# Attention head outputs turned on VectorE instead of TensorE, with part of the normalisation on GpSimd

## The reference, cut to what matters

```python
scores = jnp.einsum('bhqd,bhkd->bhqk', q, k) * SCALE      # 512 x 512 for each head
attn = jax.nn.softmax(scores, axis=-1)
out = jnp.einsum('bhqk,bhkd->bhqd', attn, v)
out = out.transpose(0, 2, 1, 3).reshape(B, Tq, C)
return out @ Wo.T + bo                                    # added to x
```

## Time and profile before

| | |
|---|---|
| median of 3 runs | 4522.98 us |
| the runs | 4522.26, 4527.35, 4522.98 us |
| span of the profiled execution | 4527.3 us |
| PE / DVE / ACT / POOL busy | 3886.3 / 3074.1 / 2057.9 / 795.1 us |
| steps of a0 (first to last exponential) | from 163.8 us to about 760 us |
| steps of a2 | from 2977 to 3393 us |
| steps of a3 | from 3836 to 4250 us |

### The profile page before, as it was taken

One profiled execution on the slowest core, in us unless ns is written; L12 is line 12 of the kernel. 1 busy time (PEld: TensorE's weight loads), 2 busy tenths in 40 slices (PEclk: granted clock), 3 DMA queues, 4 the chain that ended last, 5 costly groups with the idle time before them and its releaser, 6 DMA issues. The chain is left out here.

```text
span 4527.3 us, 83053 instructions
## 1 busy us (share of the span) xinstructions
PE 3886.3 (86%) x30431; PEld 2824.0 (62%) x30525; DVE 3074.1 (68%) x7110; ACT 2057.9 (45%) x3636; POOL 795.1 (18%) x510
## 2 busy tenths in 40 slices
PE   6799997799377999796399999779997987999899
PEld 5344443798365777575378888635555665555577
DVE  7666664456746666544566666678867887888587
ACT  3355554233103333342044444347775762777510
POOL 6433321401431000000023322410000013000000
PEclk9799999599668999897599999879998998999999
DMA  8233331201311000011054544722210015222000
GB/s 266 86 100 101 101 91 54 68 26 42 125 62 33 19 19 19 28 40 37 13 158 124 132 125 125 230 80 66 66 38 19 1 35 199 60 67 67 28 19 19
DMA packets 234478, 338.02 MB, mean 75 GB/s; under 512 B 39204, under 2 KB 132950, under 8 KB 234167
## 3 DMA queue, kind: packets, MB, share of 16 engines
q1 hardware_dynamic: 218280, 306.66, 21.4%
q0 software_dynamic: 15888, 27.23, 2.8%
HBM read 242.42 MB, written 107.01 MB: 77 GB/s over the span
## 5 line engine op out<-in xcount | busy, mean ns | idle before, releaser
L1918 ACT ACTIVATE a_pT<-a_psS 128x512 f32<-128x512 f32 x1536 | 836.0, 597 | 387.7 <-PE a_psS L1804 382.4
L1990 DVE TENSOR_REDUCE a_mx<-a_psA 128x1 f32<-128x512 f32 x1024 | 656.4, 685 | 82.9 <-PE a_psA L1782 82.8
L1819 PE MATMUL a_psZ<-a_pT,a_V 128*17 128x128 f32 x12288 | 488.8, 278 | 0.0
L1782 PE MATMUL a_psA<-a_ks,a_qs 48*128 48x512 f32 (+1 forms) x1536 | 405.5, 523 | 83.8 <-DVE a_mx L1990 36.9
L1986 DVE CUSTOM_DVE_ANT_0 a_scored<-a_psA,a_hide_q 128x512 bf16<-128x512 f32 x512 | 332.7, 688 | 184.4 <-PE a_psA L1782 183.3
L1819 PEld LDWEIGHTS a_psZ<-a_pT,a_V 128*17 128x17 f32 x12288 | 272.8, 97 | 272.7 <-issue 163.3
L1782 PEld LDWEIGHTS a_psA<-a_ks,a_qs 48*128 48x128 f32 (+1 forms) x1536 | 151.6, 192 | 330.2 <-DVE a_mx L1990 127.7
L1804 PE MATMUL a_psS<-a_qs,a_ks 50*128 50x512 f32 (+1 forms) x1536 | 318.3, 408 | 2.7 <-ACT a_pT L1918 0.8
L3262 DVE SCALAR_TENSOR_TENSOR ex_h<-ex_psU,ex_ub,ex_sg 128x512 f32<-128x512 f32 x129 | 96.9, 751 | 189.3 <-PE ex_psU L159 182.3
L2002 POOL TENSOR_TENSOR X<-X,a_osb 128x512 f32<-128x512 f32 x48 | 61.1, 1278 | 935.3 <-ACT a_osb L1905 917.3
L3208 ACT CAST ex_w_h<-X 128x1024 fp32r<-128x1024 f32 x102 | 106.0, 1040 | 149.5 <-DMA X<-in_L_ffn_gw 145.7
(11 more groups left out here) (606 smaller groups left out, 10227.2 us busy)
## 6 DMA issues: line engine op xcount, KB each, us to landing
a_qs<-a_q_parts SPq DMA_DIRECT2D x576, 64.0 KB, 2.3
a_ks<-a_k_parts SPq DMA_DIRECT2D x576, 64.0 KB, 2.3
a_k_parts<-a_p_kp SPq DMA_DIRECT2D x96, 256.0 KB, 2.6
a_q_parts<-a_p_qp SPq DMA_DIRECT2D x96, 256.0 KB, 3.2
X<-in_L_ffn_gw SPq DMA_DIRECT2D x36, 512.0 KB, 4.4
X<-in_L_ffn_up_w SPq DMA_DIRECT2D x36, 512.0 KB, 3.3
X<-in_L_ffn_down_w SPq DMA_DIRECT2D x36, 512.0 KB, 3.8
top_rows<-blank_rows SPq DMA_DIRECT2D x32, 514.0 KB, 4.8
```

What stands on the lines that cost most here:

```text
L1782: nc.tensor.matmul(psA[:, unit(a, par) % 3], qs[r, g % ring, p % 2, q * P:(q + 1) * P], ks[r, g % ring, p % 2], start=True, stop=True).the ...
L1819: last = nc.tensor.matmul(psZ[q * VP:q * VP + VW, g % 2, j * P:(j + 1) * P], V[:, b, kt, g % NG * GH + j, :], pT[:, p % 2, par, kt, q * P: ...
L1918: nc.scalar.activation(pT[:, p % 2, par, kt, :], psS[:, unit(t, par) % 3], ACT.Exp).then_inc(exp_done, 1)
L1990: nc.vector.tensor_reduce(mx[:, p // 2 % 2, par, p % 2, q:q + 1], psA[:, unit(a, par) % 3], AX_X, ALU.max).then_inc(a_used, 1)
```

## The change

The output of a group is turned by one VectorE transpose of 32x32 blocks, straight out of the `psZ` bank into SBUF (`ohT`). ACT's copy and PE's four transposes go, and with them the entry "heads" in `found`. So that a block transpose leaves each query on a partition of its own, the four column groups of `values` no longer take four runs of 128 queries: group q takes the queries i * 128 + q * 32 + c (i from 0 to 3, c from 0 to 31), four runs of 32 queries, through `tokens_of`. `take_output` runs at the same place as before (`TAKEN` = 5, ahead of the maxima of step 8g + 13). It has the transpose first; in a2 and a3 it keeps the reciprocal, and the product goes to POOL (`normalise`). In a0 the four operations stay on DVE and read SBUF instead of PSUM. New semaphores: `o_turned` (the bank is read; PE waits for it before it reuses the bank) and `on_ready` (the product is done; the "turn" waits for it, and DVE before the next transpose).

```diff
+TAKEN = TB + 1
-        oh = sb("oh", [P, GH, P])
+        ohT = sb("ohT", [P, GH, TB, VP])
-            found.append((STEPS * g + 12, STEPS * g + 12, "heads", g))
+        def tokens_of(x, q):
+            return x.rearrange("p (i q c) -> p q i c", i=TB, q=TB)[:, q]
+        def turned_before(t):
+            return max(0, min(GROUPS, (t - STEPS - TB) // STEPS + 1))
 # PE, values(t)
+                        if g >= 2:
+                            pe.wait_ge(o_turned, g - 1)
...
-                                                    pT[:, p % 2, par, kt, q * P:(q + 1) * P], start=(kt == 0), stop=(kt == TB - 1),
+                                                    tokens_of(pT[:, p % 2, par, kt], q), start=(kt == 0), stop=(kt == TB - 1),
 # PE, use(...)
+                    if t == first and turned_before(t) > 0:
+                        pe.wait_ge(o_turned, turned_before(t))
-                    elif what == "heads":
-                        pe.wait_ge(oh_ready, n + 1)
-                        for j in range(GH):
-                            last = nc.tensor.transpose(ps[:, j * P:(j + 1) * P], oh[:, j, :], G.ident[:])
                     elif what == "turn":
...
+                        pe.wait_ge(on_ready, NG * (u + 1))
 # ACT
-                        nc.scalar.copy(oh[:].rearrange("p j c -> p (j c)"), psZ[:, g % 2]).then_inc(oh_ready, 1)
 # DVE
+                def take_output(g):
+                    dve.wait_ge(o_done, GH * (g + 1))
+                    if g > 0:
+                        dve.wait_ge(on_ready, g)
+                    nc.vector.transpose(ohT[:].rearrange("p j i v -> p (j i v)"), psZ[:, g % 2]).then_inc(o_turned, 1)
+                    got = ohT[:, :, :, 0:VW]
                     if hidden is not None:
...
                         link(nc.vector.tensor_tensor(oraw[:], usum[:, u % 2, :, heads, :].rearrange("p q j v -> p j q v"), weight, ALU.mult))
+                        dve.wait_ge(o_turned, g + 1)
+                        link(nc.vector.tensor_tensor(oraw[:], oraw[:], got, ALU.add))
+                        got = oraw[:]
+                    else:
+                        dve.wait_ge(o_turned, g + 1)
+                    nc.vector.reciprocal(rden[:], got[:, :, :, DH]).then_inc(rden_ready, 1)
+                    if hidden is None:
                         return
                     dve.wait_ge(rden_ready, g + 1)
+                    nc.vector.tensor_tensor(of_heads, got[:, :, :, 0:DH], rden[:].unsqueeze(3).to_broadcast([P, GH, TB, DH]), ALU.mult
+                                            ).then_inc(on_ready, 1)
 # POOL
+                def normalise(g):
+                    pool.wait_ge(rden_ready, g + 1)
+                    nc.gpsimd.tensor_tensor(of_heads, ohT[:, :, :, 0:DH], rden[:].unsqueeze(3).to_broadcast([P, GH, TB, DH]), ALU.mult
+                                            ).then_inc(on_ready, 1)
+                if hidden is None:
+                    for g in range(GROUPS):
+                        normalise(g)
+                        if g >= NG and g % NG == 0:
+                            add_output(2 * (g // NG) - 2)
+                            add_output(2 * (g // NG) - 1)
```

More of the change, by code:

```diff
@@ L1707, in attention_by_pairs @@
         a_ready, s_ready = [sem("a_ready0"), sem("a_ready1")], [sem("s_ready0"), sem("s_ready1")]
-        a_used, max_ready, exp_done, o_done, oh_ready, rden_ready, x_full, x_free = (
-            sem(n) for n in ("a_used", "max_ready", "exp_done", "o_done", "oh_ready", "rden_ready", "x_full", "x_free"))
+        a_used, max_ready, exp_done, o_done, o_turned, rden_ready, on_ready, x_full, x_free = (
+            sem(n) for n in ("a_used", "max_ready", "exp_done", "o_done", "o_turned", "rden_ready", "on_ready", "x_full", "x_free"))
         if hidden is not None:
@@ L1891, in _ @@
                                 if n >= 4:
-                                    act.wait_ge(x_free, number["heads", n - 4] + 1)
+                                    act.wait_ge(on_ready, n - 3)
                                 nc.scalar.activation(e0[:, n % 4], mx[:, n % 2].rearrange("p r j q -> p (r j) q"), ACT.Exp,
@@ L1896, in _ @@
                             if n >= 2 * TB:
-                                act.wait_ge(x_free, number["heads", NG * (n // TB - 2) + NG - 1] + 1)
+                                act.wait_ge(on_ready, NG * (n // TB - 1))
                             nc.scalar.copy(usum[:, n // TB % 2, n % TB], bank_of(k)[:, 0:H * VW].rearrange("p (h v) -> p h v", h=H)
@@ L1943, in split_maxima @@
                                                    ALU.subtract).then_inc(max_ready, 1)
-                def take_output(g, k):
+                def take_output(g):
                     u, heads = g // NG, slice(g % NG * GH, (g % NG + 1) * GH)
-                    dve.wait_ge(x_full, k + 1)
-                    got = bank_of(k).rearrange("p (j q v) -> p j q v", j=GH, v=VP)
+                    of_heads = on[:, u % 2].rearrange("p i (h d) -> p h i d", h=H)[:, heads]
+                    dve.wait_ge(o_done, GH * (g + 1))
[3 more added lines that the diff above has]
+                    got = ohT[:, :, :, 0:VW]
                     if hidden is not None:
@@ L1970, in _ @@
                         split_maxima(t // STEPS + 1)
-                    for what, n, k in ending(t - 1, "heads"):
-                        take_output(n, k)
+                    g = t // STEPS - 1
+                    if t % STEPS == TAKEN and 0 <= g < GROUPS:
+                        take_output(g)
                     a = t + LEAD
@@ L2002, in add_output @@
                     nc.gpsimd.tensor_tensor(tiles, tiles, osb[:, n % 2].rearrange("p (q d) -> p q d", q=2), ALU.add).then_inc(out_added, 1)
-                for u in range(B):
-                    if hidden is not None and u + 1 < B:
+                def normalise(g):
+                    u, heads = g // NG, slice(g % NG * GH, (g % NG + 1) * GH)
+                    of_heads = on[:, u % 2].rearrange("p i (h d) -> p h i d", h=H)[:, heads]
+                    pool.wait_ge(rden_ready, g + 1)
[7 more added lines that the diff above has]
+                            add_output(2 * (g // NG) - 1)
+                for u in range(B if hidden is not None else 0):
+                    if u + 1 < B:
                         pool.wait_ge(x_free, number["sums", TB * u + TB - 1] + 1)
```

10 lines of the change are left out of this document (removed).

## The result

Six runs of each kernel, side by side: 4547.15 us median for the changed kernel (4541.17 to 4550.63), 4527.71 us for the kernel before (4522.26 to 4536.67). The ratio is 1.0041, 95% interval 1.0029 to 1.0053, so 13 to 24 us slower. The profiled execution spans 4541.3 us, 14.0 us more than that of before. (The median of before over six runs is 4.7 us above that of the three shown ahead of the prediction. The difference measured beside it is 19.4 us; the prediction had 29.)

The account below looks back on a forecast made before the run. DVE's stay at each group's output was taken as the bound; 12.8 us in a2 and a3 plus 17.6 in a0 minus 1 at the ends gave +29 us on 4522.98, so 4552 us, range 4520 to 4585.

Parts of the forecast that it names:

- What bounds: At each group's output in all three attentions, DVE ends PE's wait; removing PE's transposes and ACT's copy counts nothing.
- The transpose: On DVE, the added block transpose of 128x512 out of PSUM takes 0.69 us, bounded by 0.42 and 1.22 us.
- a2 and a3: the term: DVE's time for a group's output in a2 and a3 rises from 0.73 to 0.93 us: 12.8 us over 64 groups.
- a0: 0.55 us forecast: In a0 the transpose comes in front of DVE's four operations, each group 0.55 us later: 17.6 us over 32 groups.
- POOL's product: In a2 and a3 the product moved to POOL takes 0.74 us and no turn waits for it.
- The ends: At the three attention ends, the path from last values to turn shortens by 0.3, 0.3 and 0.7 us: about -1 us.
- The sum: Whole kernel: 12.8 + 17.6 - 1 = +29 us, 4552 us predicted.
- (a): Faster: PE is the bound in a0, saving 0.30 us a group there, 9.6 us: 4513 us; chance 0.12.
- (b): No change: DVE's transpose runs at twice the rate, 0.42 us: 4526 us; chance 0.10.
- (c): Slower than forecast: DVE's transpose runs at half the rate, 1.22 us; 80 us more, 4603 us; chance 0.08.
- (d): PE's values matmuls pay 10% for reading short runs, 14 us on top in a0: 4566 us; chance 0.05.
- (e): POOL and DVE block each other over SBUF in a0, one 1.28 us wait per batch, 10 us: 4562 us; chance 0.05.

Follow-up runs that it names:

- pe_refilled: Changed kernel with PE making the two maxima matmuls of each output's step three times; 4542.9 us, ratio 1.0025 to the kernel before.
- twice_refilled: Changed kernel with every block transpose made twice and PE's maxima matmuls of each output's step made three times; 4623.29 us, ratio 1.0199 to the kernel before.
- product_dve: Changed kernel with the product of a2 and a3 taken back from POOL to DVE; 4604.31 us, ratio 1.0175 to the kernel before.
- a0_old: Changed kernel with a0 put back to the way of before, so only a2 and a3 changed; 4530.92 us, ratio 1.0003 to the kernel before.
- a0_only: Changed kernel with a2 and a3 put back to the way of before, so only a0 changed; 4542.17 us, ratio 1.0033 to the kernel before.
- one_run: Changed kernel with values matmuls reading one run of 128 queries again, without the new query order; 4538.46 us, ratio 1.0009 to the kernel before.
- turn_twice: Changed kernel with every block transpose made twice, the first into an unread tile; 4667.69 us, ratio 1.0321 to the kernel before.
- spread: Changed kernel with DVE's output work in a0 spread over four steps and the turn one step later; 4538.22 us, ratio 1.0011 to the kernel before.
- spread_behind: Changed kernel with a0's DVE output work over four steps and POOL's next key mask held until the previous batch's heads are out; 4541.84 us, ratio 1.0039.

## Why the prediction was right

- **What bounds.** Right, and it is what made the sign: DVE's stay away from its maxima is what PE waits for behind each output, in a0 too, where PE has the larger share. PE's wait at its maxima matmuls grew from 46.2 to 99.7 us, and PE's transposes are covered (`pe_refilled`). (Two of the 14 waits of the earlier trace rows, of 0.20 us, stand behind a "max" and not a "turn" or "out"; nothing hangs on them.)
- **The transpose.** Forecast 0.69 us, measured 0.709. The estimate of 0.71 us from the Trainium skill, "VectorE: DVE Perf Modes", section "The three transpose paths", agrees too. On the path it costs 0.60 (`twice_refilled`), less than its duration, since operations on DVE overlap their neighbours by some 0.08 us.
- **a2 and a3: the term was mis-sized.** Forecast 0.20 us a group, 12.8 us; measured 0.04, 2.5 us. The step that failed is the gap in front: I let the transpose start 0.03 us behind the maximum, and it starts 0.08 before its end, as other operations do. The other 0.06 are the four maxima behind the reciprocal, 2.50 us against 2.56 behind a product; why they are shorter wasn't tested.
- **a0: 0.55 us forecast, 0.42 measured,** 17.6 and 13.5 us. The same start: 0.11 us of the difference. The four operations behind the transpose took about what they took before (1.60 us to the next maximum, 1.64 before).
- **POOL's product.** Forecast 0.74 us, measured 0.619; it starts 0.08 us behind the end of the reciprocal. No "turn" waited for it in the middle of an attention. Where it costs nothing, DVE would have paid: `product_dve`.
- **The ends: -1 us forecast; it is there, and drowned.** From the last values to the "turn" a3 has 4260.96 - 4259.05 = 1.91 us instead of 2.32, a2 the same, and a0 2.48 instead of 3.27: 1.6 us in all. But in the profiled executions a3's two output projections behind it ran at half rate after and at full rate before, which costs 3.6 us. The first of the two, before and after:

```profile
4251.41 1.97 PE L1862 MATMUL a_psZ<-a_wo,a_oT 128*128 128x256 f32 x8 [0.77 <-ACT a_oT L1901]
```

```profile
4264.15 3.75 PE L1867 MATMUL a_psZ<-a_wo,a_oT 128*128 128x256 f32 x8 [0.77 <-ACT a_oT L1906]
```

  That isn't the change's doing: with a3 changed, `a0_old` has them at full rate (1.97 and 1.99 us), and with a3 as before, `a0_only` at half (3.75 and 3.78). In the ends, where PE waits for each of its operands, the clock falls in some executions and not in others, so an end can't be forecast to a microsecond.
- **The sum.** +29 us forecast, 16 us by the batches, 19.4 by the medians. Sign and range held; a third of the size was too much, mostly for one reason: a gap in front of the transpose was assumed where the trace shows an overlap (0.11 us x 96 = 10.6 us). What lies between 16 and 19.4 us is within the interval.
- **The rivals.** (a), (b) and (c) fell with the transpose's 0.709 us and PE's wait, (d) with `one_run`. (e) didn't happen in the changed kernel, but that was luck of timing, by 0.3 and 0.15 us: a second transpose brings it on (`turn_twice`, `twice_refilled`), and it is what stopped `spread`. A rival was missing: that waits on PE bring its clock down. At 0.76 us behind each output they didn't (clock 1.00 from the second batch on). At 1.27 to 1.36 us they did in some batches and not in others, and a2 and a3 of `turn_twice` became 73 us longer, where DVE's time at full clock (0.60 us x 64) explains 39.

## What to carry to other kernels

Moving work off the engine with the largest share helps only where that engine ends the wait; look at the step behind the work that is moved, and at who is late there, before counting what is removed. Where an in-order engine feeds another a step ahead, its longest uninterrupted piece counts, not its sum: split it over steps, but look first at what POOL does in SBUF at those times. And a wait that is lengthened on PE can cost more than its length, when its clock falls.

## What the runs showed of the hardware

- A block transpose of 128x512 fp32 out of PSUM takes 0.71 us on DVE (0.67 when it follows another), about the time of a maximum over as much data (0.69).
- PE with a wait of 0.69 to 0.78 us behind each output (one output in 12.6 us in a2 and a3, in 19.1 in a0) kept the full clock, 1.00, from the second batch to the seventh of all three attentions. With 1.35 us behind nearly every output of a2 and a3 two of twelve batches kept it and the others fell, as far as 0.78, with single operations at the 1.2 GHz level (1.02 instead of 0.63 us, 0.80 instead of 0.50); with 1.27 us four of twelve kept it. Needless matmuls that cut the 1.35 us to 0.89 brought 1.00 back in all twelve.
- DVE operations on two inputs in SBUF were held up by POOL's single-input operation of 128x2048 until 3.7 to 3.9 us of its 5.37 had passed (484.79 - 480.85 and 490.35 - 486.41 in `spread`, 496.27 - 492.60 in `spread_behind`, 430.23 - 426.31 in `twice_refilled`); one that started 4.2 us after POOL's start ran freely. A single-input operation of 128x16 was held to POOL's end (498.00 against 497.97).
